# One decoder block on one core: the rows of x loaded in 96 and 4, the rows of h stored late in three pieces

## The reference

```python
x = x + jnp.tanh(g_xattn[0]) * _L0_xattn_ref(_layernorm(x, axis=-1), ctx_4096)
x = x + jnp.tanh(g_ffn[0]) * _L0_ffn_ref(_layernorm(x, axis=-1), W_gate, b_gate, W_e, b_e)
```

## Time and profile before

| | |
|---|---|
| median of 3 runs | 349.36 us (346.36, 354.34, 349.36) |
| profiled execution, its own time | 346.13 us |
| its span, first to last instruction | 344.2 us |
| TensorE busy in it | 316.2 us, 92% |
| mean granted TensorE clock | 0.99 |
| moved by DMA | 90.57 MB, 263 GB/s over the span |

### The profile page before, as it was taken

One profiled execution on the slowest core, in us unless ns is written; L12 is line 12 of the kernel. 1 busy time (PEld: TensorE's weight loads), 2 busy tenths in 40 slices (PEclk: granted clock), 3 DMA queues, 4 the chain that ended last, 5 costly groups with the idle time before them and its releaser, 6 DMA issues.

```text
span 344.2 us, 4282 instructions
## 1 busy us (share of the span) xinstructions
PE 316.2 (92%) x1488; PEld 231.1 (67%) x1488; DVE 203.3 (59%) x434; ACT 123.0 (36%) x165; POOL 77.7 (23%) x97
## 2 busy tenths in 40 slices
PE   0989999989999999969999999999999999999960
PEld 0554465555565588748887788888888888888840
DVE  2226368477668886895566885755176675753220
ACT  2223444346435548012544535515031551431000
POOL 6101131110213210402422331530121233111130
PEclk9999999999999999999999999999999999999996
DMA  7999999999989895218999999898469889644142
GB/s 257 309 270 333 348 352 398 392 315 385 375 302 353 303 391 170 70 54 207 398 312 397 368 354 330 237 383 258 63 178 350 269 219 390 189 61 63 18 76 30
DMA packets 24333, 90.57 MB, mean 263 GB/s; under 512 B 2898, under 2 KB 2898, under 8 KB 24302
## 3 DMA queue, kind: packets, MB, share of 16 engines
q1 hardware_dynamic: 13662, 52.86, 42.4%
q0 software_dynamic: 7504, 25.47, 27.6%
q10 hardware_dynamic: 3136, 11.83, 9.9%
HBM read 73.63 MB, written 16.52 MB: 262 GB/s over the span
## 4 chain that ended last, share of the span: by engine, by line
PE 72%; DMA 15%; DVE 6%; issue 2%; ACT 2%; POOL 1%; SPq 0%; DVEq 0%; POOLq 0%
PE ps L442 47%; PE ps L350 9%; PE ps L375 8%; DMA kT<-in_ctx_cols 7%; DMA raw<-in_L_ffn_W_e 4%; PE ps L425 4%; DVE wl L871 3%; DMA xg<-hn_rows,src_token 3%; PE ps L396 2%; PE ps L387 1%; DMA x_all<-in_x 1%; PE ps L341 1%; DVE xl L875 1%; ACT qT L601 1%; DVE stats L728 1%
## 5 line engine op out<-in xcount | busy, mean ns | idle before, releaser
L871 DVE TENSOR_TENSOR wl<-raw,wh 128x1024 fp32r<-128x1024 f32 x64 | 75.7, 1219 | 18.7 <-ACT wh L622 18.6
L442 PE MATMUL ps<-wh,xh 128*128 128x512 f32 x256 | 83.1, 401 | 1.7 <-DVE xl L875 1.7
L442 PE MATMUL ps<-wl,xh 128*128 128x512 f32 x256 | 80.7, 394 | 1.9 <-DVE wl L871 1.9
L442 PE MATMUL ps<-wh,xl 128*128 128x512 f32 x256 | 80.2, 393 | 0.0
L622 ACT ACTIVATE wh<-raw 128x1024 fp32r<-128x1024 f32 x64 | 64.0, 1052 | 29.9 <-DMA raw<-in_L_ffn_W_e 23.0
L442 PEld LDWEIGHTS ps<-wl,xh 128*128 128x128 f32 x256 | 47.8, 188 | 13.4 <-DVE wl L871 2.8
L442 PEld LDWEIGHTS ps<-wh,xl 128*128 128x128 f32 x256 | 48.0, 188 | 10.6
L1054 POOL DMA_INDIRECT out_rows<-y,dst_token x15 | 29.7, 1978 | 109.7 <-DVE y L885 100.3
L442 PEld LDWEIGHTS ps<-wh,xh 128*128 128x128 f32 x256 | 46.3, 189 | 11.3 <-DVE xl L875 2.6
L625 ACT ACTIVATE xh<-ps 128x1024 fp32r<-128x1024 f32 x16 | 16.3, 1020 | 88.8 <-PE ps L425 88.8
L350 PE MATMUL ps<-kT,qT 128*100 128x361 f32 x128 | 44.0, 496 | 1.6 <-ACT qT L601 1.3
(11 more groups left out here) (122 smaller groups left out, 237.5 us busy)
## 6 DMA issues: line engine op xcount, KB each, us to landing
raw<-in_L_ffn_W_e SPq DMA_DIRECT2D x64, 512.0 KB, 9.9
kT<-in_ctx_cols SPq DMA_DIRECT2D x16, 722.0 KB, 16.8
ctx<-in_ctx ACTq DMA_DIRECT2D x8, 1024.0 KB, 13.1
bias<-in_L_ffn_b_e SPq DMA_DIRECT2D x8, 512.0 KB, 12.5
ctx<-in_ctx ACTq DMA_DIRECT2D x8, 420.0 KB, 16.3
out_rows<-x_all POOLq DMA_DIRECT2D x8, 400.0 KB
hn_rows<-hn POOLq DMA_DIRECT2D x8, 400.0 KB
x_all<-in_x SPq DMA_DIRECT2D x7, 400.0 KB
```

The source lines that it names most:

```text
L442: mm = nc.tensor.matmul(into[:, n * HB:(n + 1) * HB], rows[:, k, :], weights[:, k, n * HB:(n + 1) * HB], start=(k == 0 and c == first), st ...
L871: nc.vector.tensor_tensor(wl[e % 2][:, k, :], raw[e % 2][:, k, :], wh[e % 2][:, k, :], ALU.subtract).then_inc(s_wl, 1)
```

## The change

It makes four edits. Each load of x (L284, L298) becomes two DMAs, one of partitions 0 to 95 and one of 96 to 99. Loads of x move one step later and stand ahead of the keys that are issued at the same wait. The eight stores of h become three: sequences 0 to 3 in iteration 6, followed by the zeros (moved from iteration 2), sequences 4 to 6 at the head of iteration 8, and sequence 7 after the last store of hn. GpSimd's wait for zeros and h moves from ahead of the third gather to ahead of the first add; the other waits on `s_hstore` count three stores in place of eight.

```diff
+        STORES = ((0, HALF_B), (HALF_B, B - 1), (B - 1, B))
...
+            Q_SPREAD = Q // 16 * 16
+            X_PARTS = [(0, Q_SPREAD), (Q_SPREAD, Q)]
+
             def load_x(b):
-                sp.dma_start(x_all[:, b, :], x[b, :, :]).then_inc(s_x[b - 1], 16)
+                for first, end in X_PARTS:
+                    sp.dma_start(x_all[first:end, b, :], x[b, first:end, :]).then_inc(s_x[b - 1], 16)
...
             load_keys(0)
             load_x(1)
             load_keys(1)
             load_x(2)
-            load_x(3)
-            sp.wait_ge(s_scores, 1)
-            load_keys(2)
-            load_x(4)
-            for b in range(2, B):
+            for b in range(1, B):
                 if b + 1 < B:
                     sp.wait_ge(s_scores, b)
+                    if b + 2 < B:
+                        load_x(b + 2)
                     load_keys(b + 1)
-                if b + 3 < B:
-                    load_x(b + 3)
                 for k in FIRST_CHUNKS.get(b + 1, ()):
                     load_weights(0, k)
...
-            def store_hidden(b):
-                pool.wait_ge(s_h, b + 1)
-                g.dma_start(out[b * Q:(b + 1) * Q, :], x_all[:, b, :]).then_inc(s_hstore, 16)
+            def store_hidden(first, end):
+                pool.wait_ge(s_h, end)
+                rows = out[first * Q:end * Q, :].rearrange("(b q) d -> q b d", q=Q)
+                g.dma_start(rows, x_all[:, first:end, :]).then_inc(s_hstore, 16)
...
                     gather_tile(0)
                     gather_tile(1)
-                store_hidden(s - 1)
+                if s == B:
+                    store_hidden(*STORES[1])
                 guess_root(s + 2, 0, 2 if s + 2 < B else 1)
                 store_normed(s - 1)
-                if s == 2:
+                if s == B:
+                    store_hidden(*STORES[2])
+                if s + 2 == B:
+                    store_hidden(*STORES[0])
                     for t in range(HALVES):
                         rows = out[N_TOK + t * P:N_TOK + (t + 1) * P, :].rearrange("p (a d) -> p a d", d=256)
                         g.dma_start(rows, zero[:, :].unsqueeze(1).to_broadcast([P, D // 256, 256])).then_inc(s_zero, 16)
-            pool.wait_ge(s_zero, 32)
-            pool.wait_ge(s_hstore, 16 * B)
             pool.wait_ge(s_hnstore, 16 * B)
             pool.wait_ge(s_tokens, 2)
             gather_tile(2)
...
             gather_first_over(0, over, over_before)
+
+            pool.wait_ge(s_zero, 32)
+            pool.wait_ge(s_hstore, 16 * len(STORES))
             add_tile(0)
```

More of the change, by code:

```diff
@@ L297, in _ @@
             for h in range(2):
-                sp.dma_start(x_all[:, 0, h * 512:(h + 1) * 512], x[0, :, h * 512:(h + 1) * 512]).then_inc(s_x0[h], 16)
+                for first, end in X_PARTS:
+                    sp.dma_start(x_all[first:end, 0, h * 512:(h + 1) * 512], x[0, first:end, h * 512:(h + 1) * 512]
+                                 ).then_inc(s_x0[h], 16)
             load_keys(0)
@@ L321, in _ @@
             sp.wait_ge(s_hn, B)
-            sp.wait_ge(s_hstore, 16 * B)
+            sp.wait_ge(s_hstore, 16 * len(STORES))
             load_bias(0)
@@ L731, in measure_query @@
                 if b > 0:
-                    dve.wait_ge(s_x[b - 1], 16)
+                    dve.wait_ge(s_x[b - 1], 32)
                 for h in range(2):
                     if b == 0:
-                        dve.wait_ge(s_x0[h], 16)
+                        dve.wait_ge(s_x0[h], 32)
                     last = measure(b, 1, h)
@@ L949, in _ @@
             split_tile(2)
-            dve.wait_ge(s_hstore, 16 * B)
+            dve.wait_ge(s_hstore, 16 * len(STORES))
             dve.wait_ge(s_hn, B)
```

## The result

The changed kernel took 357.97 us (median of 4 runs, 355.58 to 359.19), the kernel before 349.05 us beside it (4 runs). The ratio is 1.0266 with an interval of 1.0214 to 1.0318: slower by 9 us. The forecast was slower by 3 us, 352.0 with a range up to 358; its direction and its mechanism are what happened, its size is not, and the median lies inside the range by 0.03 us only. The profiled execution took 355.58 us against 346.13 before.

The account below looks back on a forecast made before the run. TensorE was taken as the bound from 9 us on. Against the profiled 346.13 us, -0.9 - 1.3 - 0.8 + 6.0 = +3.0 gave 349.1, on the median 352.4; forecast 352.0, range 345 to 358.

Parts of the forecast that it names:

- What bounds the kernel: TensorE from 9 us on: edits win only ahead of its first matmul or in its gaps; new waits are paid fully.
- x in 96 and 4 rows: Start: loads on 16 engines show the second half of x 0 near 3.9, not 4.73; 0.9 us won.
- The attention stage: Stores taken out before 100 us relieve full DMA: 1.3 us won, bounds zero to 1.4.
- worth more in ordinary runs: Rival, chance 0.08: late attention transfers explain 3.2 us between profiled run and median; 349.2 with the stall, 343 or less without.
- The late rows of x: Loads one step later, costed at nothing; rival, chance 0.05: x late by 3 us, twice, adds 4 us, giving 356.
- The wait for the gather: Turn of tile 0: stores and zeros ahead of gather 0 make TensorE stand 6.0 us in place of 0.8.
- +14.8: Gather 0's landing in us after the issue of sequence 5's hn store; TensorE comes at +8.8.
- half of the engines: Share the second expert's weights might take beside gather 0, making it up to 3 us later.
- my bound of 10: Upper bound in us of TensorE's stall at the turn of tile 0; the lower was 0.
- The half clock, a rival at 0.18: Behind the stall TensorE restarts at 1.2 GHz, costing 2.8 us: 355.2; decides from a 5 us stall on; chance 0.18.
- The other pieces, and the moved wait: Sequences 4 to 6 ahead of the last hn, and GpSimd's wait ahead of the first add: covered, no cost.
- The rival on the fast side: Gather 0 comes in time, held before only by other queues' rows; its 0.8 us gap goes: 346.4; chance 0.27.

Follow-up runs that it names:

- h5_behind: Kernel before, x loads unchanged, with GpSimd's wait moved to the first add and the store of h of sequence 5 behind the first two gathers: 348.99 us, ratio 0.998.
- h_last: Changed kernel with the zeros back in iteration 2 and all of h stored in two pieces behind the last store of hn: 344.21 us, ratio 0.9926.
- x_alone: Kernel before with only the loads of x changed (96 and 4 rows, one step later, ahead of the keys): 345.42 us, ratio 0.9959.
- store_spread: Changed kernel with each late store of h split into two DMAs, partitions 0 to 95 and 96 to 99: 356.45 us, ratio 1.0167.
- warm: Changed kernel with 100 more identity transposes on TensorE ahead of the turn of tile 0: 356.35 us, ratio 1.0175.
- weights_wait: Changed kernel with SyncE waiting for gather 0 to land before issuing the second expert's weights: 356.05 us, ratio 1.0139.
- gathers_first: Changed kernel with the store of h 0 to 3 and the zeros issued right behind the first two gathers, not ahead: 353.26 us, ratio 1.0175.
- zeros_early: Changed kernel with the zeros moved back to iteration 2: 353.74 us, ratio 1.0157.
- stores_alone: Changed kernel with x loaded as in the kernel before, leaving only the stores and the moved wait: 359.34 us, ratio 1.0354.
- piece_early: Changed kernel with the store of h 0 to 3 and the zeros issued in iteration 4 instead of 6: 357.62 us, ratio 1.0212.

## Why the prediction was wrong in its size, point by point

- **What bounds the kernel** was read rightly: a new wait of TensorE was paid in full, and no later stage made up more than 0.4 us of it. The other half of it, that a gap closed is time won, does not hold for the gap of 0.8 us at the gather: where it goes, VectorE holds TensorE for 0.7 (h5_behind, h_last).
- **x in 96 and 4 rows: mis-sized.** Forecast 0.9 us won at the start (its own working, 4.73 to 3.9, gives 0.8), measured 0.1: the second half of x 0 is seen at 4.61, was 4.73. All ten profiles with the split have 4.26 to 4.71, half of them at or under 4.51, so 0.2 us is the better figure. Here are SyncE's first issues and VectorE's first statistics after, and the DMA of the first 5 us:

```profile
0.81 1.53 SPq L307 DMA_DIRECT2D x_all<-in_x  x4
```

```profile
3.42 0.69 DVE L734 BATCH_NORM_STATS2 stats<-x_all 100x6 f32<-100x512 f32 x1 [3.42 <-DMA x_all<-in_x]
4.61 0.69 DVE L734 BATCH_NORM_STATS2 stats<-x_all 100x6 f32<-100x512 f32 x1 [0.49 <-DMA x_all<-in_x]
```

```profile
DMA packets 315, 0.84 MB, mean 169 GB/s; under 512 B 40, under 2 KB 40, under 8 KB 315
```

  The small packets are 40, as 2 x (16 + 4) has it, so the spread over all engines is real. But the last of the four DMAs is issued at 2.02 and lands 2.57 us later, for 8 KB: the time goes into the issues and a latency that I had put at 1.9 us. The Trainium skill, "DMA: Bandwidth & Descriptors", had a rule for each side (the number of engines in "Why a DMA increments its semaphore by 16 and not by 1", "Don't bother" in "Rules for kernel authors"); the 40 packets agree with the first, and the 0.1 us nearly with the second, for this transfer at least.
- **The attention stage: right in sum, by luck.** TensorE reached the turn 2.2 us earlier, as forecast (0.9 + 1.3), but not by the parts forecast. The gaps near 71, 76 and 87 us are gone. But 1.4 us of the 2.2 come from the first group of matmuls, 6.50 us against 7.92, and 0.96 us went to a wait for keys. That group takes 6.5 to 8.1 us across the profiles, 8.03 in x_alone and 8.08 in h_last, whose x 0 and first keys are loaded as in the changed kernel: the 1.4 us differ from execution to execution and can't be credited to the change. (Its matmuls take 0.81 us at the median before and 0.47 after, which the prediction read as the half clock; the granted clock reads 1.00 there from the start of both profiles, so that row doesn't show it.) The arrival scatters as much: 111.0 to 113.5 us in five profiles whose programs are alike up to 102 us and differ only in what is issued from there on (the changed kernel, store_spread, warm, weights_wait, gathers_first). What the relief of the stage is worth was not tested alone. The eight profiled kernels without the h stores of that stage, and with no other new wait ahead of the turn, arrive at 111.0 to 113.8 (median 112.6), the four that have them at 113.3 to 118.4 (median 115.0), which speaks for a gain and leaves the rival "worth more in ordinary runs" open; h_last is the only kernel here that may show some of it in its time. The late rows of x cost nothing: VectorE's waits for x were 12.0 us after, 14.1 before.
- **The wait for the gather: the step that failed.** "I take +14.8, near the faster end: TensorE stands for 14.8 - 8.8 = 6.0 us." It landed at +20.5, and TensorE stood for 11.8. The place, the queue and who waits were right; three terms of the way were too small. Rate: my bounds were 392 and 309 GB/s, and +14.8 stands for about 340; both came from stretches in which other queues were busy too, and this queue, alone, moved 276 from 105 to 111 us (store_spread: about 1.3 us of it are the 100 partitions). Sharing: "half of the engines" was two thirds, and of the 3 us that I allowed the +14.8 holds at most 1.5 (weights_wait: 2.2 us). And the price of the bytes: 1.05 MB of zeros alone were 3.9 us of way (zeros_early), or 0.27 MB per us, where 340 GB/s gives 3.1. These overlap and don't add up to the 5.7 us exactly. My own upper bounds, 15.8 and 3 more, were still 1.7 short, and the stall of 11.8 is beyond my bound of 10.
- **The half clock, a rival at 0.18, is part of what happened.** I gave it 2.8 us; it cost 1.5 in the profile of the change and up to 2.9 in others. I made it decide "from a stall of 5 us on", after the 5.0 us of the earlier trace rows; here it came 1.5 us after the last matmul and in other profiles 0.6 to 3.9, so the 5.0 us cannot be read as a threshold. Forecast and this rival belonged together: h5_behind has a fall behind a wait of 3.46 us, and in these profiles every wait of 6.5 us or more behind TensorE's first matmul has one, unless TensorE was kept at work in it (warm).
- **The other pieces, and the moved wait**: free, as forecast. TensorE waited for no gather but that of tile 0.
- **The rival on the fast side** failed: the order on GpSimd's own queue held the gather, and other queues only added to it (the 2.2 us of weights_wait). gathers_first shows it, with the same bytes in the same stretch and the gather landed in 6.7 us.

## What to carry to other kernels

A queue that carries transfers someone waits for must not carry a large one ahead of them: ask of every store that you merge or delay which small transfer now stands behind it, the double-buffer store as much as the gather. Price such a place with the rate at which that queue alone moves that shape and with its share beside the others, not with the best rate of the whole chip; and when the waiting engine is TensorE, add the half clock. The best place found for 3.3 MB here was the one behind which nothing was issued for 14 us, and even there the next gather was 1.9 us late.

## What the runs showed of the hardware that was not expected

- TensorE's granted clock fell to half at very different times after the last matmul ahead of a wait: 0.6 us (store_spread), 1.0 (stores_alone), 1.5 (the changed kernel), 2.1 (weights_wait), 3.6 (zeros_early, piece_early) and 3.9 (gathers_first), and 5.0 at the end of the run before, 2.4 at the end of the run after. Behind the wait of 3.46 us in h5_behind it fell when TensorE had already been back at work for 1.0 us. It also fell for 6.8 us in zeros_early behind a stretch where TensorE was half busy (2.08 of 4.00 us), and in some executions and not in others of the same work.
- With both queues full, SyncE's took 1.97 MB and GpSimd's 0.98 MB in 8 us (the changed kernel, 115 to 123 us).
- The stores of several sequences in 100 partitions came with extra small packets. The count under 512 B is 2898 before and 2988 with x split (9 x (20 - 10) more, as it should be), but 3244 in the changed kernel, where five stores fewer should have made it 2908; with the stores in 96 and 4 partitions it is 2956, as the count of DMAs has it. In h_last, with two stores of four sequences, it is 3276, 384 more than the count of DMAs gives: 48 for each sequence in such a store, in both kernels, and none for the store of a single one. What these packets are is open; they were seen beside the low rate, and that they cause it was not tested.
